# Moving the sum, inverse and scaling of a softmax total into the next block, with one more chunk added on GpSimd, earlier token loads and a reordered prologue

## The reference

```python
imp = softmax(band_importance)[0];  _, idx = top_k(imp, 3)      # three masked key columns
q, k, v = x@Wq.T + bq, x@Wk.T + bk, x@Wv.T + bv                  # heads of 32
attn = softmax(q k^T / sqrt(32) + bias)                          # 2048 x 2048 per head
y = x + (attn v) @ Wo.T + bo
x1 = layernorm(x + layernorm(y)*gamma + beta)
h = x1 @ Hadamard(512);  hq = 4-bit quantised h (per row)
out = layernorm(x1 + hq @ ternary(W_ffn).T)
```

## Time and profile before

| | us |
|---|---|
| median of 3 runs | 5198.88 (5195.54 to 5202.60) |
| the profiled execution, its own time | 5202.82 |
| its span, first to last instruction | 5201.0 |
| PE busy | 4825.8 (93%) |
| POOL busy | 4000.7 (77%) |
| DVE busy | 3336.5 (64%) |
| ACT busy | 2581.0 (50%) |

### The profile page before, as it was taken

The page is one execution under the profiler, slowest core; times in us unless marked ns, Lnnn a source line. Parts: engine busy times, 40 slices in busy tenths (PEclk is TensorE's granted clock), DMA queues, the critical chain, the costliest instruction groups (busy, mean ns, idle before and its releaser), DMA issues.

```text
span 5201.0 us, 83024 instructions
## 1 busy us (share of the span) xinstructions
PE 4825.8 (93%) x23512; PEld 2380.7 (46%) x23512; DVE 3336.5 (64%) x5886; ACT 2581.0 (50%) x4891; POOL 4000.7 (77%) x1295
## 2 busy tenths in 40 slices
PE   6999999998899999999879999999988999999967
PEld 3444444443544444444444444444444444444424
DVE  5476666665766666666557666666666666666727
ACT  0455555553555555555345555555534555555535
POOL 1598888886479888888648988888865888888875
PEclk7999999999999999999989999999999999999988
DMA  4412233224411333322341223322333223332112
GB/s 116 96 38 58 60 69 64 57 62 100 119 29 39 64 70 66 70 58 64 101 106 38 44 62 68 64 58 62 70 114 78 42 47 65 70 66 56 37 44 72
DMA packets 247640, 346.24 MB, mean 67 GB/s; under 512 B 16529, under 2 KB 102289, under 8 KB 247186
## 3 DMA queue, kind: packets, MB, share of 16 engines
q1 hardware_dynamic: 247186, 340.73, 28.8%
HBM read 205.33 MB, written 33.55 MB: 46 GB/s over the span
## 4 chain that ended last, share of the span: by engine, by line
PE 63%; issue 11%; POOL 8%; DMA 7%; DVE 6%; ACT 2%; SPq 1%; POOLq 0%; DVEq 0%; ACTq 0%
PE ps_m L490 18%; PE ps_s L505 16%; PE ps_o L532 14%; DMA qst<-lo 5%; POOL acc L1032 4%; PE ps_m L477 3%; DVE umax L844 3%; PE ps_z L451 3%; PE ps_z L445 3%; PE ps_z L510 2%; ACT prob L701 1%; SPq L290 1%; DVE lo L813 1%; PE ps_s L566 1%; POOL prob L1058 1%
## 5 line engine op out<-in xcount | busy, mean ns | idle before, releaser
L1032 POOL TENSOR_TENSOR acc<-acc,prob 128x2048 f32<-128x2048 f32 x704 | 3216.7, 4569 | 68.2 <-ACT prob L701 2.2
L844 DVE TENSOR_REDUCE umax<-ps_m 128x1 f32<-128x512 f32 x4096 | 2523.3, 682 | 806.9 <-PE ps_m L490 806.7
L701 ACT ACTIVATE prob<-ps_s 128x512 f32<-128x512 f32 x4096 | 2123.8, 602 | 1355.8 <-PE ps_s L505 1305.9
L505 PE MATMUL ps_s<-qst,kst 99*128 99x512 f32 x4096 | 1714.3, 435 | 131.5 <-ACT prob L701 81.4
L490 PE MATMUL ps_m<-kst,qst 97*128 97x512 f32 x4096 | 1693.9, 423 | 30.3 <-DMA qst<-lo 27.0
L505 PEld LDWEIGHTS ps_s<-qst,kst 99*128 99x128 f32 x4096 | 761.6, 190 | 1184.1 <-ACT prob L701 679.1
L532 PE MATMUL ps_o<-prob,vst 128*32 128x512 f32 x8192 | 1099.1, 609 | 0.0
L490 PEld LDWEIGHTS ps_m<-kst,qst 97*128 97x128 f32 x4096 | 781.1, 191 | 462.4 <-DVE umax L844 317.9
L1016 POOL TENSOR_TENSOR obuf<-obuf,zinv 128x512 f32<-128x512 f32 x64 | 82.4, 1287 | 560.7 <-DVE zinv L856 560.7
L1032 POOL TENSOR_TENSOR acc<-prob 128x2048 f32<-128x2048 f32 x64 | 292.8, 4575 | 285.1 <-ACT prob L701 285.1
L856 DVE RECIPROCAL zinv<-ps_z 128x512 f32<-128x512 f32 x64 | 214.9, 3358 | 405.3 <-PE ps_z L510 405.3
(11 more groups left out here) (112 smaller groups left out, 2397.6 us busy)
## 6 DMA issues: line engine op xcount, KB each, us to landing
xk<-in_xT_dram SPq DMA_DIRECT2D x66, 1024.0 KB, 5.6
xq<-in_xT_dram SPq DMA_DIRECT2D x65, 1024.0 KB, 8.7
kst<-hi SPq DMA_DIRECT2D x128, 256.0 KB, 6.8
qst<-hi SPq DMA_DIRECT2D x128, 256.0 KB, 5.6
wq<-in_wT_dram SPq DMA_DIRECT2D x65, 256.0 KB, 9.0
kst<-lo SPq DMA_DIRECT2D x64, 256.0 KB, 5.7
qst<-lo SPq DMA_DIRECT2D x64, 256.0 KB, 6.8
ctxT_dram<-obuf SPq DMA_DIRECT2D x64, 256.0 KB, 2.4
```

The lines of the kernel that those rows point to most:

```text
L505: nc.tensor.matmul(ps_s[:, (i * HG * NKC + HG * c + h) % NSB, :], kst[i // NQB % 2][0:RALL, h, c * P:(c + 1) * P], qst[i % 2][0:RALL, h, : ...
L701: nc.scalar.activation(prob[:, c % NPB, h, :], ps_s[:, (i * HG * NKC + HG * c + h) % NSB, :], ACT.Exp, scale=SCALE).then_inc(ex, 1)
L844: nc.vector.tensor_reduce(umax[:, m, kb:kb + 1], ps_m[:, u % NMB, :], AX.X, ALU.max).then_inc(mred, 1)
L1032: nc.gpsimd.tensor_tensor(acc[:], a, prob[:, c % NPB], ALU.add).then_inc(padd, 1)
```

## The change

1. `PE_SUMS` becomes `[14, 15]`: POOL adds chunk 9 too, 13 additions for each block where there were 12, and the PE sums two chunks.
2. The total of block n-1 is computed by the PE in block n, behind the product of chunk `TOTAL_CHUNK` = 1. DVE takes the reciprocal ahead of the first unit of chunk 2. POOL normalises block n-1 behind the first addition of block n. Only block 15 of a batch still has its own total at its end.
3. `KEY_CHUNK`, `VALUE_CHUNK` go from 2, 5 to 4, 7.
4. The parameters and the first two token tiles are loaded during block 15, not behind its stored context. gamma, beta and bo move to slots of `prob`, and two output tiles with them. The PE's waits for the last `zrec`, `oz_cp` and `mcp` move from the start of the token phase to its step 2. The loads of the next batch's queries move to that step.
5. Prologue: keys and queries of both first stages come first, with the ternary steps of DVE between them, and the maxima last. The weights of the feed-forward part are loaded behind xk.

```diff
-PE_SUMS = [9, 14, 15]
-KEY_CHUNK, VALUE_CHUNK = 2, 5
+PE_SUMS = [14, 15]
+KEY_CHUNK, VALUE_CHUNK, TOTAL_CHUNK = 4, 7, 1
...
+            def total(n):
+
+                pe.wait_ge(padd, n * NADD + 2 * NADD)
+                column_sums(acc, False, True).then_inc(zdone, 1)
...
                     mm.then_inc(pv, 1)
+                    if i > 0 and c == TOTAL_CHUNK:
+                        total(n - 1)
...
-                pe.wait_ge(padd, n * NADD + 2 * NADD)
-                column_sums(acc, False, True).then_inc(zdone, 1)
+                if i == NBLK - 1:
+                    total(n)
...
             def maxima(f, i=0, last=False):
                 for u in range(UNITS):
+                    if i > 0 and u == units_at[TOTAL_CHUNK + 1][0][0]:
+                        inverse_sums(f - 2)
...
-                        inverse_sums(n)
+                        if i == NBLK - 1:
+                            inverse_sums(n)
...
                     nc.gpsimd.tensor_tensor(acc[:], a, prob[:, c % NPB], ALU.add).then_inc(padd, 1)
+                    if k == 0 and i > 0:
+                        normalise(n - 1, i - 1)
...
-                        if i > 0:
-                            normalise(n - 1, i - 1)
-                        attend(n)
+                        attend(n, i)
...
+            def load_first_tiles(b, n, last):
+                load_projection(n, IC - 1)
                 for t in range(2):
-                    sp.wait_ge(k_stk[t], (b * NG + NG + (0 if last else 1)) * (2 * NSTK))
+                    wait_alone(sp, k_stk[t], (b * NG + NG + (0 if last else 1)) * (2 * NSTK), passed)
                 wait_alone(sp, q_stk, (b * NBLK + NBLK + (0 if last else 2)) * NSTK, passed)
+                wait_alone(sp, cst, b * (NBLK * 16) + NBLK * 16, passed)
+                for t in range(2):
+                    load_rows(b, t)
+                    load_context(b, t)
...
             keys(0)
             queries(0)
+            keys(1, 1)
+            queries(1)
+            ternary()
...
             for u in range(UNITS):
                 unit(u, 0, 0, 0)
             maxima_to_rows(0, first=True)
-            queries(1)
-            keys(1, 0)
```

More of the change, by code:

```diff
@@ L49 @@
 NST = 3
+PARAMS = (IC + 3) * 16
+PAR_SLOT = 4
 KEY_STEP = NT - 1
@@ L164, in build @@
         tHT = [rows[:, 12 + t, :] for t in range(2)]
-        tO = [rows[:, r, :] for r in (17, 18, 19)]
+        tO = [rows[:, r, :] for r in (14, 15, 19)]
         tQ = rows[:, 20, :]
@@ L367, in store @@
                     sp.dma_start(out[bass.ds(b * L + t * P, P), :], tO[t % NST]).then_inc(c_st[t % NST], 16)
[L369 to L372, removed]
                 for s in range(-1, STEPS):
                     with step_of(sp, b) as bb:
+                        if s + 3 == NT - QB // P:
+                            wait_alone(sp, cst, bb * (NBLK * 16) + (NBLK + 1) * 16, passed)
+                        if s == 2 and not last:
+                            next_queries(bb, NBLK + 1)
                         if 0 <= s + 1 < NT - 2:
@@ L420, in batch @@
                             queries(n + 2, (n >> 4) & (NB - 1), i + 2)
+                        if i < NBLK - 2 or i == NBLK - 2 and not last:
+                            next_queries((n >> 4) & (NB - 1), i + 2)
+                        if i == NBLK - 1:
+                            load_first_tiles((n >> 4) & (NB - 1), n, last)
                         store_context(n, i, (n >> 2) & (NS - 1))
@@ L621, in tokens, with ternary @@
                     pe.wait_ge(v_cp, b * (NG * NQB) + (NG + 2) * NQB)
[L624 to L627, removed]
-                for oc in range(IC):
[L629 to L635, removed]
+            def ternary():
+                pe.wait_ge(idf, 5)
+                pe.wait_ge(tern_ok, 1)
+                for c in range(IC):
+                    for oc in range(IC):
+                        nc.tensor.transpose(ps_tern[c].bitcast(BF16)[:, oc * P:(oc + 1) * P],
+                                            ternb[:, oc, c * P:(c + 1) * P], identb[:])
+                for oc in range(IC):
+                    mm = nc.tensor.matmul(ps_o[:, oc * P:(oc + 1) * P], ones[:], diag[:, oc * P:(oc + 1) * P],
+                                          start=True, stop=True)
+                mm.then_inc(tern_t, 1)
             pe.sem_inc(pv, NKC)
@@ L786, in _ @@
             queries(0, 0)
+            keys(1, 1, 1)
+            act.wait_ge(k_stk[0], 2 * (2 * NSTK))
+            queries(1, 1)
             maxima_rows(0)
-            queries(1, 1)
-            keys(1, 1, 0)
             def batch(b, last):
@@ L814, in low_part, with keys @@
                                                       in1=high.bitcast(F32), op0=ALU.add, op1=ALU.subtract)
-            def keys(stage, s, n=None):
+            def keys(stage, s, q=None, between=None):
                 for t in range(NQB):
-                    if t == 0 and n is not None:
-                        dve.wait_ge(q_stk, (n + 2) * NSTK)
+                    if t == 0 and q is not None:
+                        dve.wait_ge(q_stk, q * NSTK)
                     dve.wait_ge(k_hi, stage * NQB + t + 1)
@@ L823, in keys @@
                     low_part(lo[:, t % 2], hi[:, t % 2], 1, s).then_inc(k_lo, 1)
+                    if between is not None:
+                        between(t)
             def queries(f, k):
@@ L982, in _ @@
+            dve.wait_ge(bias_ld, 16)
+            dve.sem_inc(zrec, 1)
+            keys(0, 0, between=ternary)
+            queries(0, 0)
+            keys(1, 1, 1)
+            queries(1, 1)
             dve.wait_ge(tern_t, 1)
```

123 lines of the change are left out of this document (69 added, 54 removed).

## The result

The changed kernel takes 5522.48 us (median of four executions), the kernel before 5197.28 in the same rounds: the ratio is 1.0622, with a 95% interval of 1.0601 to 1.0643. Three of the four took 5519.29 to 5524.79 us; the fourth took 12744.84 us at a granted clock of 0.363 and is left out of the ratio. It is 6% slower. I had forecast 5312 and a range up to 5385: the direction was right, the size far too small. The profiled execution took 5524.79 us, with a span of 5523.0.

A forecast was written before the change was run, and what follows sets the result against it. A ring of POOL, PE and DVE was taken to bound plain blocks, PE the projecting ones. Blocks +191, token loads -54 and prologue -24 made +113 on 5202.8, 5315.8 profiled, 5312 as median; range 5235 to 5385 us.

The forecast's parts named there:

- Part 1: Plain blocks: scaling hidden, but a thirteenth addition and a handover of 6.75 us through chunk 1; ring 69.3 us against 62.7.
- Part 2: Projecting blocks: PE loses a 0.86 us pass, the reciprocal delays chunk 2 by 2.77; 70.3 us against 68.4.
- Block sum: All blocks of the four batches, from first addition to final total: +133 and +58, together +191 us.
- Part 3: Token loads at batch ends: first product sooner, -12 us for each of three batches and -18 in the last, -54.
- Part 4: Prologue: the first key product no longer waits for the ternary steps; -24 us, bounds -35 and -10.
- C: Rival, chance 0.15: the clock falls at each plain seam, +4 us at each, +76 in all, 5388 us.
- B: Rival, chance 0.15: the reciprocal does not stop PE, POOL's ring of 69.3 us rules everywhere; -41, 5271 us.
- D: Rival, chance 0.10: the handover does decouple, plain ring 63.8 us and projecting block 67.5; about 5096 us.
- E: Rival, chance 0.05: both gains at the ends fail, +191 alone, less 20; 5370 us.

The follow-up runs named there:

- e5: The changed kernel with a reciprocal of only 64 of 512 columns, seven eighths of the inverse left out: 5304.69 us.
- e6: The changed kernel with the total of the block before one chunk earlier, behind chunk 0's value products, and the reciprocal ahead of chunk 1's units: 5329.43 us.
- e2: The changed kernel with PE summing chunk 9 again, so that POOL makes 12 additions and not 13: 5465.37 us.
- e4: The changed kernel with the third unit of chunk 2 computed nine times over, extra PE work where PE would stand still: 5388.36 us.
- e3: The changed kernel with the reciprocal in four pieces of 128 columns between units and the scaling behind POOL's second addition: 5342.59 us.
- e7: e1 with the thirteenth addition in all blocks, the sum, inverse and scaling left where they were before: 5188.42 us.
- e1: The kernel before with only the change's early token loads and reordered prologue; additions, total and projections as before: 5125.12 us.
- e10: The changed kernel with a reciprocal of 256 of 512 columns, half of the inverse left out: 5329.06 us.
- e8: e1 with thirteen additions in projecting blocks and twelve in plain ones: 5098.82 us.

## Why the prediction was wrong

**Part 1, the ring of a plain block: right.** 70.2 us as a mean of 15 against 69.3, and e5, e6 and the one plain block of e2 without a dip confirm its pieces, each within about 0.3 us. What is above 69.3 goes with the clock at the seam, since the idle is 6.68 us where it does not fall there. Worth +14 us in the sum of errors.

**Part 2, projecting blocks: the step that failed.** It said 68.4 - 0.86 + 2.77 = 70.3. The mean of the 41 is 74.7, 4.4 us more, or +180 of the +210 us that the forecast missed. The usual block takes 75.0, 4.7 us more, and this splits into two terms that were left out:

- *The clock, 3.9 us.* The step took PE's stop at its length and did not ask what the clock does behind it. e4 prices it: 75.0 with the stop, 71.1 with PE busy in it. e3 agrees from the other side, 70.03 and 72.97 us for one list of instructions at clock 1.00 and 0.95.
- *The wait for the query rows, 0.8 us.* At full clock the block would still take 71.0 to 71.1, not 70.3 (e2's 71.9, less the sum of chunk 9; e4). The total no longer stands ahead of chunk 1, so PE reaches its first unit sooner, and waits there for the copies of `qst`: 9.9 us in nine blocks of batch 1, against 2.2 before. What the removed pass gave was taken back there. I read this from the waits of the two traces and did not isolate it by a run.

```profile
PE ps_m L517 <- DMA qst<-lo: 9.9, 9, 1.2
```

(the waits of PE after, blocks from 1700 to 2500: us in total, times, longest)

The rest of the sum holds: 68.4 - 0.86 = 67.5 is the block with thirteen additions and the total in its old place, and e7 has 67.6. The stop itself was rightly called: 2.25 us of idle, where I had 2.77.

**Block sum.** +391 measured, +191 forecast. Of the 200 between, 180 belong to the projecting blocks and 14 to the plain ones; the last 6 are blocks 0 and 15 of the batches.

**Part 3, token loads:** forecast -54 (three times -12, and -18). From final total to the next batch's first addition the seams shortened by 10.5 each, the last end by 16.8: -48. **Part 4, prologue:** forecast -24, the first addition came 21.2 us sooner. Together -69 against -78, and e1's 5125 shows them by themselves.

**The rivals.** C had the mechanism and the wrong place. I looked for the clock's fall where PE's time to spare is largest, at the plain seams, and priced it at 5388. There it does happen, and POOL's ring hides all but 0.9 us of it. In the projecting blocks, where PE is the bound and every lost cycle counts, I had counted a stop of 2.8 us and stopped thinking. The Trainium skill, "TensorE: Matmul & The Clock Gate", in its section "Why this matters for your kernels", advises against idle gaps of PE between bursts of matmuls, from a length on that this stop does not reach; by that alone a stop of 2.25 us would have been harmless. The trace does not bear this out: behind the stop of 2.25 us, with a wait of about 1.1 some 7 us before, the granted clock was 0.50 in every projecting block of batches 1 and 2. The measurement decides. The same page, in "A second HAM failure mode: psum-queue depth-cycling", tells of a kernel that cycles through its PSUM banks and in which short idles between groups of matmuls make the clock swing; e10's fall behind a wait of 1.24 us is of that kind, and this is the rule that I should have weighed against Part 2. B (no stop) is refuted by the 2.25 us in the rows. D (decoupled) is refuted by the idle of 7.4 us. E is refuted by e1.

The reason that the design loses is then told in three lines. It wanted to hide 1/z and the scaling behind the next block. The reciprocal of 3.36 us was hidden before, beside chunk 0, which has no units; now it stands ahead of units, at the place where DVE has 0.47 us to spare. And POOL's handover now runs through chunk 1 and is longer than the one it replaced (7.4 against 4.76). The thirteenth addition adds to this in the plain blocks: made everywhere, it costs 63 us over e1 (e7).

What stays open is which sum of short waits makes the clock fall. The rows tell where it falls: behind the stop in all 41 projecting blocks of the change and of e6, in 31 of e2, and in none of e3, e4, e5 and e10; and at the seam in some blocks of e2, e3, e4, e5 and e10. They do not tell why the same waits bring a fall in one block and none in the next, as in e10, or why two stops of e2 without an earlier fall brought none.

## What to carry to other kernels

When a change makes a busy TensorE wait, price the wait twice: its length, and the granted clock behind it; where TensorE sets the pace the second can be the larger (here 2.25 us of idle cost 3.9 more). A long instruction of another engine is cheap only at a place where nobody waits for that engine: move it with its neighbours in view, or cut it into pieces. And where a kernel has two kinds of block with different bounds, apply a trade between engines only to the kind that it helps (the thirteenth addition, on top of e1: about 26 us gained where it was made in the projecting blocks alone, e8, and 63 lost where it was made everywhere, e7).

## What the runs showed of the hardware

- An idle of 2.25 us between matmuls, in a TensorE stream that was otherwise busy over 90%, was followed by some 10 us at a granted clock of 0.50, though the engine was busy 9.83 of those 10.
- Filling that stop with matmuls (e4: idle 0.45 us) left no fall there in 41 blocks; the change had one in all 41.
- In e10 a fall of 7 us followed a wait of only 1.24 us, with 0.38 and 0.23 beside it; the same wait in the block before had none. In e3 one followed waits of 0.68 and 0.75 us. In the kernel before, idles of 1.15 us at the plain seams left blocks at 1.00.
- Eight matmuls whose result is thrown away, 1.99 us of work in a stop of 2.25, made a kernel of 5522 us 134 us faster (e4).
